# Query and key parts stored by place in the six pairs, and loaded with one DMA over 96 partitions

## The reference, cut to what matters

```
q = heads(xn @ Wq + bq);  k = heads(xn @ Wk + bk)        # (b, h, 512, 16)
pos_emb = dist_emb[pos_l - pos_r + 255]                  # (l, r, 16)
scores = q·k + einsum('bhld,lrd->bhlr', q, pos_emb) + einsum('bhrd,lrd->bhlr', k, pos_emb)
probs = softmax(scores / 4)
```

## Time and profile before

| | |
|---|---|
| median of three runs | 1908.28 us (1906.44 to 1913.13) |
| profiled execution: span from first to last instruction | 1907.4 us |
| mean granted TensorE clock | 0.914 of full speed |
| PE busy | 1569.2 us, 82% |
| VectorE, ScalarE, GpSimd busy | 1251.0, 1042.0, 571.0 us |
| moved by DMA | 510.58 MB |
| stages in the trace | project 0 to 126, route 126 to 343, experts 343 to 1247, attention 1247 to 1907 us |

### The profile page before, as it was taken

How to read it: one execution, slowest core, us unless ns; L and a number is a source line. 1 busy time by engine, 2 the same in 40 slices (tenths; PEclk the granted TensorE clock), 3 DMA queues, 4 the chain that set the end, 5 groups by cost and what they waited for, 6 DMA issues and landing times. The chain is left out here.

```text
span 1907.4 us, 35518 instructions
## 1 busy us (share of the span) xinstructions
PE 1569.2 (82%) x12086; PEld 1183.0 (62%) x12086; DVE 1251.0 (66%) x3122; ACT 1042.0 (55%) x2242; POOL 571.0 (30%) x760
## 2 busy tenths in 40 slices
PE   5758640586999988988999899749999999998996
PEld 3324420485988878977898789625555555555553
DVE  6747454450465646655666566749888888888895
ACT  2425220122655545544555455249888888888883
POOL 1342338141010011111101000013354555635556
PEclk9878665698999999999999999969999999999998
DMA  6554427768698789899999888689989999899991
GB/s 214 174 181 127 122 94 234 198 177 273 233 349 287 262 293 359 284 320 343 367 336 363 273 295 302 255 262 328 321 266 312 313 311 317 278 334 294 286 324 46
DMA packets 227286, 510.58 MB, mean 268 GB/s; under 512 B 38209, under 2 KB 84801, under 8 KB 222625
## 3 DMA queue, kind: packets, MB, share of 16 engines
q1 hardware_dynamic: 202144, 410.57, 66.2%
q0 software_dynamic: 23808, 93.54, 14.2%
q10 hardware_dynamic: 1152, 4.19, 0.6%
HBM read 435.11 MB, written 195.82 MB: 331 GB/s over the span
## 5 line engine op out<-in xcount | busy, mean ns | idle before, releaser
L986 DVE TENSOR_TENSOR rel_out<-rl,rel_tile 128x1024 f32<-128x1024 f32 x256 | 401.2, 1572 | 289.9 <-PE rl L1039 220.6
L963 ACT COPY rel_tile<-rl 128x1024 f32<-128x1024 f32 x256 | 259.3, 1017 | 279.3 <-DVE rel_out L986 197.3
L1288 ACT ACTIVATE scores<-scores,row_least 128x512 f32<-128x512 f32 x512 | 365.6, 717 | 46.8 <-DVE row_least L1324 46.7
L1324 DVE CUSTOM_DVE_ANT_1 scores<-sc,rq 128x512 f32<-128x512 f32 x512 | 337.9, 686 | 72.7 <-issue 64.7
L1449 PE MATMUL pt<-ident,scores 128*128 128x128 f32 x2048 | 323.0, 281 | 27.8 <-ACT probsT L1295 23.7
L1449 PEld LDWEIGHTS pt<-ident,scores 128*128 128x128 f32 x2048 | 249.7, 145 | 111.3 <-DVE probsT L1332 40.4
L1059 PE MATMUL up<-rowsT,w_b 128*128 128x128 f32 x2272 | 294.3, 286 | 13.5 <-issue 6.2
L1059 PEld LDWEIGHTS up<-rowsT,w_b 128*128 128x128 f32 x2272 | 276.9, 199 | 15.4 <-DVE rowsT L992 8.4
L1070 PE MATMUL dn<-w_b,hid 128*128 128x256 f32 x1136 | 273.2, 385 | 0.0
L971 ACT ACTIVATE hid<-up,w_b 128x128 f32<-128x128 f32 x568 | 162.1, 369 | 174.7 <-PE up L1059 174.4
L1441 PE MATMUL sc<-ks,qs 96*128 96x512 bf16 x512 | 204.8, 400 | 35.8 <-DMA ks<-scratch_parts 20.4
(11 more groups left out here) (197 smaller groups left out, 1695.8 us busy)
## 6 DMA issues: line engine op xcount, KB each, us to landing
scratch_rel<-rel_out SPq DMA_DIRECT2D x256, 512.0 KB, 4.3
rq<-scratch_rel SPq DMA_DIRECT2D x256, 512.0 KB, 8.6
w_b<-in_w POOLq DMA_DIRECT2D x71, 1152.0 KB
w_b<-in_w POOLq DMA_DIRECT2D x71, 1028.0 KB
krows_sb<-scratch_stack SPq DMA_DIRECT2D x768, 64.0 KB, 3.4
scratch_parts<-part SPq DMA_DIRECT2D x96, 128.0 KB
qrows_sb<-scratch_stack SPq DMA_DIRECT2D x192, 64.0 KB, 3.1
qs<-scratch_parts SPq DMA_DIRECT2D x192, 64.0 KB
```

Source lines behind the costliest of these rows:

```text
L963: nc.scalar.copy(dst, src).then_inc(s_kc, 1)
L986: nc.vector.tensor_tensor(out[n % SRING][:], rl[r][:].rearrange("p a (b s) -> p (a b) s", s=TILE), square(tile)[:, u * UN:(u + 1) * UN], A ...
L1288: nc.scalar.activation(sm[j][:, i], sm[j][:, i], ACT.Exp, bias=least[:, j, i:i + 1], scale=-1.0, accum_out=es[:, g // 2 % 2, i, 2 * j + g ...
L1324: nc.vector.tensor_tensor_reduce(sm[j][:, i].rearrange("p (c s) -> p c s", c=LT), sc[i % 2][:].rearrange("p (c s) -> p c s", c=LT), rq[j][ ...
```

## The change

Where each part is used is now stored where it is used. `parts` becomes `pairs` (side, 96, batch and head, row): each part of a query is stored once for each pair it belongs to, under each other in the order of the pairs, and so are those of the keys. In `project` that is still 12 stores a batch, 6, 4 and 2 after the three parts, each now of 256 KB. The order of the pairs is new, so that places 0 to 2 hold three different parts on either side. `by_head` loads these places with two DMAs over 48 partitions each. `stack` gets all six places of either side too: its two stores become 12 in each of the two stages (`STACKED`), together 12 MB in place of 6 MB. A piece of keys, a piece of queries, a group's `qs` and its `ks` are then one DMA over 96 partitions each. The columns of Wq, Wk and their biases are reordered on the host, so that a partition of the product is a dimension and a pair of heads, and a partition's 2 KB lie together in `pairs`. The masks that split the tables follow the new order.

```diff
-PAIRS = [(0, 0), (0, 1), (0, 2), (1, 0), (1, 1), (2, 0)]
+PAIRS = [(0, 2), (1, 1), (2, 0), (0, 1), (1, 0), (0, 0)]
+BASE = D * PARTS
+STACKED = ((0, 0, BASE, 0), (1, 0, BASE, BASE), (0, BASE, 2 * D, 0), (1, BASE, 2 * D, BASE + D), (0, BASE + 2 * D, D, 0), (1, BASE + 2 * D, D, BASE + 2 * D))
...
-        mask = sb("mask_sb", [KS, 2])
+        mask = sb("mask_sb", [KS, 2, 2])
...
-                    for c in range(4):
-                        at = b * H + (c % 2) * (H // KC)
-                        dst = t["parts"][c // 2 * PARTS + k, :, at:at + H // KC].rearrange("d h s -> h d s")
-                        sp.dma_start(dst, part[b % PRING][k][:, c]).then_inc(s_ps[b % PRING], 16)
+                    for n, pair in enumerate(PAIRS):
+                        for side in range(2):
+                            if pair[side] == k:
+                                dst = t["pairs"][side, n * D:(n + 1) * D, b * H:(b + 1) * H].rearrange("d (h c) s -> d h c s", c=KC)
+                                sp.dma_start(dst, part[b % PRING][k][:, 2 * side:2 * side + 2]).then_inc(s_ps[b % PRING], 16)
...
-                src = t["parts"].rearrange("q d h s -> (q d) h s")[:, b * H:(b + 1) * H, 0:2 * TILE]
-                sp.dma_start(by_head[b % 2][:], src).then_inc(s_bh[b % 2], 16)
+                for side in range(2):
+                    src = t["pairs"][side, 0:BASE, b * H:(b + 1) * H, 0:2 * TILE]
+                    sp.dma_start(by_head[b % 2][side * BASE:(side + 1) * BASE], src).then_inc(s_bh[b % 2], 16)
...
-                dst = t["stack"][i].rearrange("q d l h -> (q d) l h")
-                sp.dma_start(dst, by_row[:, i * TILE:(i + 1) * TILE]).then_inc(s_bs, 16)
-            sp.wait_ge(s_bs, 16 * 2)
+                for side, at, rows, src in STACKED:
+                    sp.dma_start(t["stack"][i, side, at:at + rows], by_row[src:src + rows, i * TILE:(i + 1) * TILE]).then_inc(s_bs, 16)
+            sp.wait_ge(s_bs, 16 * 2 * len(STACKED))
...
-                for i, pair in enumerate(PAIRS):
-                    src = t["stack"][tile % LT, PARTS + pair[0], :, p * PIECE:(p + 1) * PIECE]
-                    sp.dma_start(kst[x % KRING][i * D:(i + 1) * D], src).then_inc(s_kl[x % KRING], 16)
+                sp.dma_start(kst[x % KRING][:], t["stack"][tile % LT, 1, :, p * PIECE:(p + 1) * PIECE]).then_inc(s_kl[x % KRING], 16)
...
-                for i, pair in enumerate(PAIRS):
-                    src = t["stack"][lt, pair[0], :, p * PIECE:(p + 1) * PIECE]
-                    sp.dma_start(qst[i * D:(i + 1) * D, p], src).then_inc(s_ql[p], 16)
+                sp.dma_start(qst[:, p], t["stack"][lt, 0, :, p * PIECE:(p + 1) * PIECE]).then_inc(s_ql[p], 16)
...
-                    for n, pair in enumerate(PAIRS):
-                        src = t["parts"][side * PARTS + pair[side], :, g * HG:(g + 1) * HG]
-                        sp.dma_start(dst[i][n * D:(n + 1) * D], src).then_inc(s_qk[i], 16)
+                    sp.dma_start(dst[i][:], t["pairs"][side, :, g * HG:(g + 1) * HG]).then_inc(s_qk[i], 16)
...
+    def by_dim(w):
+        return w.reshape(w.shape[:-1] + (H // KC, KC, D)).swapaxes(-3, -2).swapaxes(-2, -1).reshape(w.shape)
...
-        "Wq": a["L0_attn_Wq"], "Wk": a["L0_attn_Wk"], "Wv": a["L0_attn_Wv"],
+        "Wq": by_dim(a["L0_attn_Wq"]), "Wk": by_dim(a["L0_attn_Wk"]), "Wv": a["L0_attn_Wv"],
...
-    for name, shape, dt in (("parts", (2 * PARTS, D, BH, S), BF16), ("stack", (LT, 2 * PARTS, D, TILE, BH), BF16),
+    for name, shape, dt in (("pairs", (2, KS, BH, S), BF16), ("stack", (LT, 2, KS, TILE, BH), BF16),
```

More of the change, by code:

```diff
@@ L308, in split_table @@
                 tab.settle()
-                tab.did(nc.vector.scalar_tensor_tensor(tmp32[:], tabh[:], mask[:, 0:1], tab32[:, i], ALU.mult, ALU.add))
+                tab.did(nc.vector.scalar_tensor_tensor(tmp32[:], tabh[:], mask[:, i, 0:1], tab32[:, i], ALU.mult, ALU.add))
                 tab.settle()
@@ L312, in split_table @@
                 tab.settle()
-                tab.did(nc.vector.scalar_tensor_tensor(dst[:], tabh[:], mask[:, 1:2], tmp32[:], ALU.mult, ALU.add))
+                tab.did(nc.vector.scalar_tensor_tensor(dst[:], tabh[:], mask[:, i, 1:2], tmp32[:], ALU.mult, ALU.add))
                 tab.settle()
@@ L537, in repack @@
             def repack(b):
-                act.wait_ge(s_bh[b % 2], 16 * (b // 2 + 1))
+                act.wait_ge(s_bh[b % 2], 32 * (b // 2 + 1))
                 nc.scalar.copy(*repacked(b)).then_inc(s_ba, 1)
@@ L651, in repack @@
             def repack(b):
-                dve.wait_ge(s_bh[b % 2], 16 * (b // 2 + 1))
+                dve.wait_ge(s_bh[b % 2], 32 * (b // 2 + 1))
                 nc.vector.tensor_copy(*repacked(b)).then_inc(s_bd, 1)
@@ L871, in load_k @@
                 tile, p = x // PIECES, x % PIECES
-                for i, pair in enumerate(PAIRS):
-                    src = t["stack"][tile % LT, PARTS + pair[0], :, p * PIECE:(p + 1) * PIECE]
-                    sp.dma_start(kst[x % KRING][i * D:(i + 1) * D], src).then_inc(s_kl[x % KRING], 16)
+                sp.dma_start(kst[x % KRING][:], t["stack"][tile % LT, 1, :, p * PIECE:(p + 1) * PIECE]).then_inc(s_kl[x % KRING], 16)
             def load_q(lt, p):
-                for i, pair in enumerate(PAIRS):
-                    src = t["stack"][lt, pair[0], :, p * PIECE:(p + 1) * PIECE]
-                    sp.dma_start(qst[i * D:(i + 1) * D, p], src).then_inc(s_ql[p], 16)
+                sp.dma_start(qst[:, p], t["stack"][lt, 0, :, p * PIECE:(p + 1) * PIECE]).then_inc(s_ql[p], 16)
             for b in range(B):
                 after(sp, s_br, b - 1)
-                src = t["parts"].rearrange("q d h s -> (q d) h s")[:, b * H:(b + 1) * H, 2 * TILE:4 * TILE]
-                sp.dma_start(by_head[b % 2][:], src).then_inc(s_bh[b % 2], 16)
+                for side in range(2):
+                    src = t["pairs"][side, 0:BASE, b * H:(b + 1) * H, 2 * TILE:4 * TILE]
+                    sp.dma_start(by_head[b % 2][side * BASE:(side + 1) * BASE], src).then_inc(s_bh[b % 2], 16)
             for x in range(KRING):
@@ L890, in _ @@
             for i in range(2):
-                dst = t["stack"][2 + i].rearrange("q d l h -> (q d) l h")
-                sp.dma_start(dst, by_row[:, i * TILE:(i + 1) * TILE]).then_inc(s_bs, 16)
-            sp.wait_ge(s_bs, 16 * 2)
+                for side, at, rows, src in STACKED:
+                    sp.dma_start(t["stack"][2 + i, side, at:at + rows], by_row[src:src + rows, i * TILE:(i + 1) * TILE]).then_inc(s_bs, 16)
+            sp.wait_ge(s_bs, 16 * 2 * len(STACKED))
             for p in range(PIECES - 1):
@@ L955, in relative @@
                         if tile == 0 and u == 0:
-                            act.wait_ge(s_bs, 16 * 2)
+                            act.wait_ge(s_bs, 16 * 2 * len(STACKED))
                         if tile:
@@ L1022, in relative @@
                         if u % PER_PIECE == 0:
-                            pe.wait_ge(s_kl[x % KRING], (x // KRING + 1) * 16 * len(PAIRS))
+                            pe.wait_ge(s_kl[x % KRING], (x // KRING + 1) * 16)
                     else:
                         if u % PER_PIECE == 0 and rt == 0:
-                            pe.wait_ge(s_ql[u // PER_PIECE], (lt + 1) * 16 * len(PAIRS))
+                            pe.wait_ge(s_ql[u // PER_PIECE], (lt + 1) * 16)
                     if STEP_OF[side, tile, u] >= 2:
@@ L1438, in score @@
                 if j == 0 and i == 0:
-                    pe.wait_ge(s_qk[g % 2], (g // 2 + 1) * 16 * 2 * len(PAIRS))
+                    pe.wait_ge(s_qk[g % 2], (g // 2 + 1) * 16 * 2)
                 after(pe, s_su, n * ST + i - 1)
@@ L1556 @@
     wo = a["L0_attn_Wo"].reshape(2, 2, 4, D, E).transpose(0, 2, 1, 3, 4)
-    mask = np.array([[-(p[1] > 0), -(p[1] > 1)] for p in PAIRS], np.float32).repeat(D, axis=0)
+    mask = np.array([[[-(p[i] > 0), -(p[i] > 1)] for i in (1, 0)] for p in PAIRS], np.float32).repeat(D, axis=0)
+    def by_dim(w):
+        return w.reshape(w.shape[:-1] + (H // KC, KC, D)).swapaxes(-3, -2).swapaxes(-2, -1).reshape(w.shape)
     cols = ["L0_ffn_g1", "L0_ffn_be1", "L0_ffn_g2", "L0_ffn_be2", "L0_attn_bv"]
@@ L1568 @@
         "tri": np.triu(np.ones((P, P), np.float32), 1), "turn_no": np.arange(NBLK, dtype=np.float32),
-        "bqk": np.stack([a["L0_attn_bq"], a["L0_attn_bk"]]).reshape(2 * KC, P).T,
+        "bqk": by_dim(np.stack([a["L0_attn_bq"], a["L0_attn_bk"]])).reshape(2 * KC, P).T,
         "cols": np.stack([a[n].reshape(KC, P) for n in cols]).transpose(2, 0, 1),
```

## The result

The changed kernel took 1929.16 us (median of 4 runs, 1922.98 to 1930.13), the kernel before beside it 1908.73 (4 runs, 1906.44 to 1913.13). The ratio is 1.0098, with a 95% interval of 1.0069 to 1.0127: slower by 1%, a small loss but clear of noise. The forecast was 1893, faster, in a range of 1868 to 1918. In a later repetition the ratio was 1.009 (1.0058 to 1.0122).

A forecast was written before the change was run, and what follows sets the result against it. With PE 82% busy, cheaper DMA pays only where PE, or VectorE in step, waits for data. Terms -1 + 12 + 5 - 18 - 13 = -15 us against 1907.4 gave 1892.4, 1893 as median; range 1868 to 1918.

The forecast's parts named there:

- Project, -1: End of project: the last 24 stores, doubled to 6.3 MB, change the time by -1 us, between -4 and +4.
- the rule on the split: Project: a DMA uses the largest number up to 16 dividing both outermost dimensions, 8 before, 16 after; so -4 us.
- Route, +12: End of route: stack stores of twice the bytes make the stage end at 354 us for 342, +12.
- which the slack hides: Route: at 326 GB/s the stores take 38.6 us, end at 328, and the 18.9 us SP waits afterwards absorb it: 0.
- the 5 us that I gave to GpSimd's last writes: Route: GpSimd's last small writes, stuck behind the store packets, end the stage later, +20 in place of +15.
- Start of experts, +5: Experts up to block 10: earlier stack stores of 12.6 MB delay two row loads, 21.8 us, less 17.6, plus tail: +5.
- the 17.6 us that I gave back at once: Start of experts: PE's waits for late rows (11.0) and new weights (6.6) vanish with stores issued at about 407 us.
- Steady experts, -18: Experts, steady: SP's issuing lag in tiles 3, 7 and 11 goes; -18 us, between 0 and the 50.8 of VectorE's waits.
- PE's 17.6 us of long waits: Steady experts: six long PE waits from 702.00 to 1092.74 us, taken as the size of the gain, since PE sets the pace.
- Attention, -13: Attention: two issues replace 12 loads; -4.6 us at the start and -8 in later groups, together -13, between -4 and -25.
- 4.6 us at the first tile: Start of attention: two issues take 0.9 us for 5.5, so VectorE's first tile starts 4.6 us sooner, whole.
- the slower rival: Second copy costs most: route +20, start of experts +15, gains halved to -9 and -6; 1927 us, chance 0.15.

The follow-up runs named there:

- wide: The changed kernel with the same 12 MB a stage of stack stores, as four stores over 96 partitions in place of 12; 1929.63 us, ratio 1.0068.
- stack3: The changed kernel with each part stored once in stack and a piece loaded with three DMAs in place of one; 1885.42 us, ratio 0.984.
- after: The changed kernel itself, against the kernel before; 1929.16 us, ratio 1.0098.

## Why the prediction was wrong, step by step

- **Project, -1: +1.2, inside its bounds.** The share went from 56.3% to all 16 engines, as the rule on the split had it, but its -4 did not come. Over all traces route starts at 125.7 to 128.5 us with the changed stores (seven traces) and at 126.3 to 129.0 with those of before (ten): nothing to be told apart.
- **Route, +12: +31.1, outside my 0 to +20. The step that failed first.** The pace was right: I took twice 33.9, 67.8 us, and it is 67.7. What failed is "which the slack hides", and with it the 5 us that I gave to GpSimd's last writes behind the stores. The stores end at 358.5, where I had 357, and the stage 16.7 us after that. SP's 18.9 us after its stores were in part GpSimd still issuing (until 334.0), with a DMA queue that kept up (its clears landed in 2.5 us). With the longer stores GpSimd issues until 337, but its packets take turns with SP's and get through about 9 us after the stores, and the 7.5 us in which nothing moves come on top. Stores that hold these writes up have no slack before them.
- **Start of experts, +5: +22.5, outside -17.6 to +15.** The stores went out 70 us into the stage, where I had 64. But I let 12.6 MB pass at 326 GB/s, 38.6 us; they took until about 520, 74 us. So four blocks had late rows for the two in the sum. And the 17.6 us that I gave back at once were not the issuing's: with one load and no second copy 3 to 5 came back. The experiments add up to nearly the measured number, -5 by the issues, +11 by the bytes in wide stores (wide against stack3), +15 by their going out as 12 narrower ones (after against wide). But this split is not shown: wide's trace is a fast one, and behind six loads a piece the bytes in wide stores alone cost 22. What holds is that the second copies, stored as the change stores them, cost 24 to 28 us there (157.1 and 159.0 against 131.4 and 133.0), and that wide stores would cost less.
- **Steady experts, -18: -22.8.** Right in mechanism; PE's 17.6 us of long waits are a little less than what SP's lag cost. VectorE's waits are 6.0 us for 50.8, and the kernel with one load and nothing else has this gain (24 to 28 us).
- **Attention, -13: -12.1 in the first pair of traces, but the mechanism was not this.** I had 4.6 us at the first tile, "whole"; it was 0.5. The data was late, not the issue: the first load of `rq` goes out 1.8 us into the stage for 6.4, and VectorE's first tile starts 9.4 us after it for 5.3. The engines, which I had standing idle meanwhile, are 78% busy from 1 to 11 us into the stage before, and 96% after; over its first 50 us they move 310 and 324 GB/s. On one and the same chip the whole gain is 4 to 9 us. Had I judged this step by one pair of traces, it would have passed.

So the slower rival's mechanism was the right one, at 31 and 22.5 us where it had 20 and 15, while the gains it had halved came whole. That its 1927 is next to the measured 1929 is luck: its costs were 19 us too low and its gains 20. I held two things against it. The slack was none, and the earlier issue did not help, since the stores were twice as long. It decides when the stores take over 60 us, and they took 67.7 in route. The sum of my own terms should have warned me: I had the 67.8 us and their end at 357, and the rows of GpSimd, and put them side by side as if they used different engines.

## What to carry to other kernels

Before counting the time behind a transfer as slack, ask whether what ends it is on the same DMA engines: then a longer transfer holds it up, and it ends after it. Storing data a second time to save issues must be weighed at the place where it is stored; here three loads of unlike width from a single copy gave the whole gain (0.984, and 0.9827 again) that one load from a double copy lost. And look at the outermost extent of both sides of a DMA when a layout is changed: at 2 or 3 it costs more than all the issues that it saves.

## What the runs showed of the hardware that I had not expected

- A load with an outermost extent of 2 or 3 ran on 2 or 3 engines, at 52 and 79 GB/s, and held up the stores behind it in the same queue (19.9 and 17.3 us to landing for 4.3); the kernel took 1.45 and 1.26 times as long.
- SP's issue of a stack store took 3.2 us on average in route (38.96 us for 12), and 0.47 in experts (5.65 for 12), for the same stores. With 4 KB packets it took 5.2 in route (62.35 for 12). What holds it, I did not find.
- A single pair of traces can be off by as much as the effect: the changed attention code took 648.3 to 663.3 us, that of before 655.6 to 662.0.
